# Experts of the last stage in two token halves, the first amid the quantised attention; gates by Tanh and Exp; queries per token tile

## The reference

```python
scores = sigmoid(x_flat @ w_gate); _, topk_idx = top_k(scores, 6)
w = picked scores / their sum
h_r = silu(g_r) * v_r            # g_r, v_r: the halves of x @ w_up of an expert
routed = sum over the 6 of (h_r @ w_down) * w     # tokens beyond an expert's 128th get 0
x = layernorm(x + silu(g_s) * y_s @ w_shared_down + routed)
```

## Time and profile before

| | before |
|---|---|
| three timed runs, median (lowest to highest) | 472.29 us (471.53 to 473.58) |
| span of the profiled execution | 473.8 us |
| the profiled execution's own time | not given by the page apart from its span |
| PE matmul busy / DVE / ACT / POOL | 388.1 / 303.7 / 215.5 / 118.4 us |
| mean granted TensorE clock | 0.879 |

### The profile page before, as it was taken

One profiled execution on the slowest core, in us unless ns is written; L12 is line 12 of the kernel. 1 busy time (PEld: TensorE's weight loads), 2 busy tenths in 40 slices (PEclk: granted clock), 3 DMA queues, 4 the chain that ended last, 5 costly groups with the idle time before them and its releaser, 6 DMA issues.

```text
span 473.8 us, 6810 instructions
## 1 busy us (share of the span) xinstructions
PE 388.1 (82%) x2387; PEld 225.7 (48%) x2387; DVE 303.7 (64%) x611; ACT 215.5 (45%) x551; POOL 118.4 (25%) x215
## 2 busy tenths in 40 slices
PE   5996969389987999999754867768676998999993
PEld 2645457244434566576532223333344544665572
DVE  4984498959624697878646979989871362132235
ACT  2664221272235765855214789899881311111100
POOL 8248646828460000000080111212110000000002
PEclk9989895779988899999985589998975698999997
DMA  8992110670000000000000999999982004011211
GB/s 244 318 361 25 1 2 1 223 310 1 0 1 0 1 3 0 2 1 1 2 0 13 265 169 172 155 163 173 131 162 51 0 0 143 24 44 49 63 44 44
DMA packets 75521, 39.84 MB, mean 84 GB/s; under 512 B 64160, under 2 KB 71264, under 8 KB 75040
## 3 DMA queue, kind: packets, MB, share of 16 engines
q1 hardware_dynamic: 73184, 39.35, 34.1%
q0 software_dynamic: 2304, 0.07, 1.4%
HBM read 21.58 MB, written 2.88 MB: 52 GB/s over the span
## 4 chain that ended last, share of the span: by engine, by line
PE 53%; DVE 15%; DMA 12%; ACT 10%; issue 5%; POOL 4%; SPq 0%; POOLq 0%; ACTq 0%; DVEq 0%
PE ps L762 27%; ACT area_b L692 7%; PE ps L1162 6%; DMA area_b<-area_b 6%; PE ps L945 5%; PE ps L956 5%; PE ps L975 3%; DMA area_a<-area_b 3%; POOL deltas L490 2%; PE ps L939 2%; DMA area_b<-deltas 1%; DVE area_a L1275 1%; DMA deltas<-entry_w,small 1%; ACT area_a L673 1%; DVE stats L1282 1%
## 5 line engine op out<-in xcount | busy, mean ns | idle before, releaser
L1535 DVE CUSTOM_DVE_ANT_0 area_a<-ps,zero,small 128x1024 f32<-128x1024 f32 x64 | 79.4, 1278 | 9.7 <-ACT area_b L692 5.0
L692 ACT ACTIVATE area_b<-area_a,small 128x1024 int16<-128x1024 f32 x64 | 73.0, 1142 | 11.3 <-DMA area_b<-area_b 5.9
L673 ACT ACTIVATE area_a<-ps,small 128x256 f32<-128x256 f32 (+1 forms) x128 | 51.9, 432 | 31.0 <-DVE small L1426 28.7
L459 POOL TENSOR_SCALAR var_eps<-meanvar 128x1 f32<-128x1 f32 x24 | 6.6, 273 | 225.3 <-DVE meanvar L1283 225.2
L762 PE MATMUL ps<-xT_odd,early 128*128 128x512 f32 x128 | 59.5, 613 | 0.0
L1054 PE MATMUL ps<-area_b 128*128 128x512 bf16 x128 | 45.0, 446 | 13.5 <-DVE small L1535 12.4
L1593 DVE TENSOR_TENSOR area_b<-ps,area_b 128x512 f32<-128x512 f32 x16 | 11.1, 691 | 55.7 <-ACT area_b L737 55.7
L1426 DVE TENSOR_REDUCE small<-ps 128x4 f32<-128x1024 f32 (+1 forms) x24 | 29.3, 1222 | 18.3 <-PE ps L945 18.1
L737 ACT ACTIVATE area_b<-ps 128x512 f32<-128x512 f32 x16 | 9.5, 596 | 67.2 <-PE ps L762 67.2
L762 PE MATMUL ps<-area_b,xT_even 128*128 128x512 f32 x64 | 31.1, 631 | 9.0 <-ACT area_b L650 9.0
L762 PEld LDWEIGHTS ps<-xT_odd,early 128*128 128x128 f32 x128 | 25.0, 197 | 27.1 <-issue 26.6
(11 more groups left out here) (265 smaller groups left out, 667.4 us busy)
## 6 DMA issues: line engine op xcount, KB each, us to landing
early<-in_w_up_dram SPq DMA_DIRECT2D x1, 4096.0 KB, 16.1
area_b<-gates_out SPq DMA_DIRECT2D x16, 256.0 KB, 3.0
deltas<-area_b SPq DMA_DIRECT2D x1, 2112.0 KB, 17.8
area_b<-deltas SPq DMA_DIRECT2D x2, 1024.0 KB, 5.9
area_a<-in_w_down_dram SPq DMA_DIRECT2D x1, 2048.0 KB, 8.5
early<-in_ctxT_dram SPq DMA_DIRECT2D x1, 1024.0 KB, 13.1
early<-in_ctx_dram SPq DMA_DIRECT2D x1, 1024.0 KB, 14.0
early<-in_w_qkv_dram SPq DMA_DIRECT2D x2, 384.0 KB, 5.1
```

The source lines that it names most:

```text
L673: a = act.activation(p1[:, n % 2, x * nk * P:(x + 1) * nk * P], scores1(n)[:, x * nk * P:(x + 1) * nk * P], ACT.Exp, bias=nmx1[:, n % 2, x ...
L692: act.activation(px[:, u % PX, :], sx[:, u % 3, :], ACT.Exp, bias=nbx[:, u:u + 1], accum_out=zx[:, i, h:h + 1]).then_inc(sem("px_ready"), 1)
L1535: dve.tensor_tensor_reduce(sx[:, u % 3, :], bank(2 * (u % 2), 2), zero[:].broadcast_to([P, B * M]), qsc[:, i, h:h + 1], LOWEST, ALU.add, A ...
```

## The change

- **Experts.** The 16 groups are done twice, for tokens 0 to 255 and 256 to 511, so there are 32 groups `k`, each with `up` of four matmuls of 256 columns (both halves in one bank, 4 or 5) and `down` of two (bank 3). They have fixed places in a list of 104 steps that goes on from stage 5's 64 units: `up` of the first half at steps 42 to 57, its `down` at 53 to 68; the second half at 74 to 89 and 84 to 99. In its step PE does the scores, `apply`, the previous tile's division and router, then `down`, then `up`. One step after its `up` follow ACT's tanh and DVE's `combine`, two instructions into a ring `raw_up` of eight. The product with the spread gates (`hide`) goes to POOL, from step 52 on, behind that step's bias.
- **Banks.** Since bank 3 is taken, scores of units from 48 on use three banks: bank 1 is shared by neighbours, so the second score matmul of a unit waits for the maximum of the unit before.
- **Functions.** silu(x) becomes x/2 (1 + tanh(x/2)) with ACT's Tanh, sigmoid 1/(1 + exp(-x)) with ACT's Exp and two DVE instructions. The router works tile by tile, each 10 to 15 steps after the tile's last unit.
- **Queries** are made tile by tile: tile 0's amid stage 4's items, tile 1's product right behind them, the rest of tile 1's and those of tiles 2 and 3 amid the first 17 units (tile 3's copy at 32). Tile 2's and 3's end of stage 4 moves there too. `qTx` is cleared at the kernel's start; `qstack` is made by one DVE instruction per tile.
- **DMA.** `w_down` is loaded at step 42. The gates of a half are stored (step 47, and after the units) and spread by four DMAs of 512 KB each (step 49, and after the units). SP waits for the store in its list, between the transpositions. Units 40, 49 and 58 are no longer transposed by PE and ACT; units 62 and 63 are.

```diff
-AHEAD = 6
...
+W = 2 * P
+UNITS = 64
+NARROW = 48
+UP_AT = (42, 74)
+DOWN_AT = (53, 84)
+HIDE_AT = 52
+RAW = 8
+STEPS = 104
...
         def by_scalar(u):
-            return u % SHARE[1] in SHARE[0]
+            return (u < UP_AT[0] - 3 and u % SHARE[1] in SHARE[0]) or u >= UNITS - 2
+        def halves5(u):
+            if u < NARROW:
+                return 2 * (u % 2), 2 * (u % 2) + 1
+            return u % 2, u % 2 + 1
...
+                def spread_gates(p):
+                    sp.wait_ge(sem("gates_stored"), 16 * (p + 1))
+                    for q in range(4):
+                        if p:
+                            sp.wait_ge(sem("hidden_ready"), NG // 4 * (q + 1))
+                        rows = gates_out[p][:, NG // 4 * q * W:NG // 4 * (q + 1) * W]
+                        sp.dma_start(gate_rows[:, NG // 4 * q:NG // 4 * (q + 1), :].rearrange("p g n -> p (g n)"),
+                                     rows.unsqueeze(0).broadcast_to([HE, EG, NG // 4 * W])).then_inc(sem(f"gate_rows_{q}"), 16)
+                def store_gates(p):
+                    sp.wait_ge(sem("gate1T_ready"), p + 1)
+                    sp.dma_start(gates_out[p].rearrange("e (g n) -> g e n", n=W), gate1T).then_inc(sem("gates_stored"), 16)
+                for u in range(UNITS):
...
+                    if u == 42:
+                        sp.wait_ge(sem("o1_ps"), len(items1) // 2)
+                        load("w_down", w_down, t["w_down"].rearrange("(g p) d -> p g d", p=P))
+                    if u == 47:
+                        store_gates(0)
+                    if u == 49:
+                        spread_gates(0)
+                store_gates(1)
+                spread_gates(1)
...
+            def hide(k):
+                p, g = divmod(k, NG)
+                pool.wait_ge(sem("gated_ready"), k + 1)
+                pool.wait_ge(sem(f"gate_rows_{g // (NG // 4)}"), 16 * (p + 1))
+                if k >= 2:
+                    pool.wait_ge(sem("hidden_used"), k - 1)
+                pool.tensor_tensor(out=hidden[:, k % 2, :], in0=raw_up[:, k % RAW, :], in1=gate_rows[:, g, :],
+                                   op=ALU.mult).then_inc(sem("hidden_ready"), 1)
...
+                        add_bias(u // 2 - 4)
+                    if u >= HX and u % HX == 8:
+                        inverse_deviation(5, u // HX - 1)
+                    if HIDE_AT <= u:
+                        hide(u - HIDE_AT)
+                for k in range(UNITS - HIDE_AT, NG):
+                    hide(k)
+                inverse_deviation(5, TT - 1)
+                for i in range(2):
+                    inverse_deviation(6, i)
+                for k in range(NG, 2 * NG):
+                    hide(k)
+                for i in range(2, TT):
+                    inverse_deviation(6, i)
...
+            def tanh_of(k):
+                act.wait_ge(sem("up_ps"), k + 1)
+                if k >= 2:
+                    act.wait_ge(sem("tanh_used"), k - 1)
+                act.activation(tanh_up[:, k % 2, :], bank(4 + k % 2)[:, W:2 * W], ACT.Tanh, scale=0.5).then_inc(sem("tanh_ready"), 1)
...
-                act.activation(score1.rearrange("p i e -> p (i e)"), bank(7)[:, 0:TT * E1], ACT.Sigmoid).then_inc(sem("score1_ready"), 1)
...
-                    act.activation(silu[:, g % 2, :], bank(g % 2), ACT.Silu).then_inc(sem("silu_ready"), 1)
...
+                    if n in (7, 19):
+                        project(n // 12)
+                    if n in (10, 22):
+                        transpose_x(4, [n // 12])
+                    if n == 12:
+                        queries(0)
+                    if n == 15:
+                        turn_queries(0)
                     if n and n % 2 == 0:
                         apply(n // 2 - 1)
-                turn_z(TT - 1)
-                spread_z(TT - 1)
-                project(TT - 1)
+                queries(1)
+                turn_z(2)
...
+                    two = [0, 1] if u < NARROW or u % 2 == 0 else [1, 0]
+                    for order, half in enumerate(two):
+                        if u < NARROW and u >= 2:
+                            pe.wait_ge(sem("maxx_ready"), u - 1)
+                        if u >= NARROW:
+                            pe.wait_ge(sem("maxx_ready"), u - 1 if order == 0 and u >= NARROW + 2 else u)
+                        mm = pe.matmul(bank(halves5(u)[half]), qTx[:, i % 2, h // 2, P * (h % 2):P * (h % 2) + P],
                                        kTx[:, h // 2, half * 512:(half + 1) * 512], start=True, stop=True)
                     mm.then_inc(sem("sx_ps"), 1)
...
+                def up(k):
+                    p, g = divmod(k, NG)
+                    if k < 2:
+                        pe.wait_ge(sem("pTx_act"), before5(UNITS - 2, True))
+                    else:
+                        pe.wait_ge(sem("gated_ready"), k - 1)
...
+                    rows = slice(P * g, P * (g + 1))
+                    dense(bank(4 + k % 2)[:, 0:W], lambda c: w_up[:, c, 1, rows], tokens(p))
+                    dense(bank(4 + k % 2)[:, W:2 * W], lambda c: w_up[:, c, 0, rows], tokens(p)).then_inc(sem("up_ps"), 1)
...
+                def down(k):
+                    p, g = divmod(k, NG)
+                    pe.wait_ge(sem("hidden_ready"), k + 1)
+                    if g == 0:
+                        pe.wait_ge(sem("in_w_down"), 16)
+                        pe.wait_ge(sem("maxx_ready"), NARROW)
+                        if p:
+                            pe.wait_ge(sem("res6_ready"), 2)
+                    for i in range(2):
+                        mm = pe.matmul(bank(3)[:, i * D:(i + 1) * D], hidden[:, k % 2, i * P:(i + 1) * P], w_down[:, g, :],
+                                       start=g == 0 and i == 0, stop=g == NG - 1, skip_group_check=True)
+                    mm.then_inc(sem("proj6" if g == NG - 1 else "hidden_used"), 1)
+                    if g == 0:
+                        pe.wait_ge(sem("shared_ready"), p + 1)
+                        for i in range(2):
+                            pe.matmul(bank(3)[:, i * D:(i + 1) * D], shared[:, i * P:(i + 1) * P], w_sd[:],
+                                      start=False, stop=False, skip_group_check=True)
...
+                    if u in (49, 81):
+                        share(0 if u == 49 else 1)
+                    for k in range(2 * NG):
+                        if down_step(k) == u:
+                            down(k)
+                    for k in range(2 * NG):
+                        if up_step(k) == u:
+                            up(k)
...
+                def combine(k):
+                    dve.wait_ge(sem("tanh_ready"), k + 1)
+                    if k >= RAW:
+                        dve.wait_ge(sem("hidden_ready"), k - RAW + 1)
+                    STT(out=raw_up[:, k % RAW, :], in0=tanh_up[:, k % 2, :], scalar=1.0, in1=bank(4 + k % 2)[:, W:2 * W],
+                        op0=ALU.add, op1=ALU.mult).then_inc(sem("tanh_used"), 1)
+                    dve.wait_ge(sem("tanh_used"), k + 1)
+                    TTN(out=raw_up[:, k % RAW, :], in0=bank(4 + k % 2)[:, 0:W], in1=raw_up[:, k % RAW, :],
+                        op=ALU.mult).then_inc(sem("gated_ready"), 1)
+                def add_6(p):
+                    dve.wait_ge(sem("proj6"), p + 1)
+                    for i in (2 * p, 2 * p + 1):
+                        TTN(out=res[:, i, :], in0=bank(3)[:, D * (i % 2):D * (i % 2) + D], in1=x_tok[1][:, i, :],
+                            op=ALU.add).then_inc(sem("res6_ready"), 1)
...
+                for u in range(STEPS):
+                    if u + 2 < UNITS:
+                        maximum(u + 2)
+                    if u == 0:
+                        take_z(2)
+                    if u == 1:
+                        normalise(2)
+                    if u == 2:
+                        add(2)
+                        norm_stats(4, 2)
+                    if u == 3:
+                        norm_scale(4, 2)
+                        quantise_queries(1)
+                    if u == 4:
+                        take_z(3)
+                        stack_queries(1)
+                    if u == 5:
+                        normalise(3)
+                    if u == 6:
+                        add(3)
+                        norm_stats(4, 3)
+                    if u == 7:
+                        norm_scale(4, 3)
...
+                            norm_scale(5, i)
+                        if k == 11:
+                            route(i)
+                        if k == 14:
+                            gate(i)
+                    if u in (50, 82):
+                        share(0 if u == 50 else 1)
+                    for k in range(2 * NG):
+                        if up_step(k) + 1 == u:
+                            combine(k)
+                    if u == 73:
+                        add_6(0)
+                        scale_6(0)
+                add_6(1)
+                scale_6(1)
```

(81 more changed lines are left out.)

673 lines of the change are left out of this document (330 added, 343 removed).

## The result

| | before | after |
|---|---|---|
| median of the timed runs (lowest to highest) | 472.45 us (471.53 to 473.58, 4 runs) | 491.49 us (488.86 to 492.98, 4 runs) |
| span of the profiled execution | 473.8 us | 487.1 us |
| mean granted TensorE clock in it | 0.879 | 0.892 |

After takes 1.040 times as long, with a 95% interval of 1.035 to 1.044: slower. Forecast were 456 us, with a range of 441 to 478.

The account below looks back on a forecast made before the run. It took PE to bind in stage 4 and behind the units, DVE, ACT and DMA in stage 5, with a gap between. Terms summed to -15.9 from the 473.8 span, 457.9; 1.5 lower for the median, 456 us, range 441 to 478.

Parts of the forecast that it names:

- Second half ... 16 x (1.72 + 0.86) = 41.3: Second half's ups and downs at PE's pace; with shared expert, gates and waits 49 us for 96.3 before, -47.3.
- the ring's loop: From step 53, maximum, score, apply, down, hide, combine and next maximum form a loop of 4.7 us a step.
- lock-step, slower: Rival, chance 0.12: each up's result needed in its own step, 6 us a step, steps 42 to 57 take 102, total 497.
- Steps 42 to 57, 61 us: Units with first-half ups and downs among them: 61 us for 22.6 before, +38.4.
- 58 to 63, 14: Last units' steps: one more ring step, tile 2's router, maxima and last exponential, 14 us for 13.4, +0.6.
- the ring hardly binds: Rival, chance 0.20: PE and DVE run further ahead, steps 42 to 57 take 49 us instead of 61, total 442.
- Units 0 to 41, +12.3 and +7.4: Units 0 to 15: 35 us for 22.7 before; units 16 to 41: 43.5 us for 36.1, from added query and router work.
- Start, -22.6: Gap between stage 4 and the units filled: first maximum at 238 us, 22.6 us earlier.
- no table load: Steps 42 to 57: Tanh shares Exp's set, so no loads; rival with loads, chance 0.05, +13 to +21, 475 us.
- w_down and the spread gates in time: Steps 42 to 57 and second half: DMAs stay beneath, 40 of 61 us; w_down hidden but for 0.5.
- last unit to last tile: Behind the units, to the transposed last tile: PE and ACT transpose, 11.4 us for 13.7 before, -2.3.
- tail: Kernel's end: two tiles' norms instead of four, 6 us, -2.4.

Follow-up runs that it names:

- e1: After with the semaphore count that POOL's product waits on put right in the second half; 479.06 us, ratio 1.010.
- e2: After with a ring of 16 instead of eight, the count left as it was; 485.75 us, ratio 1.026.
- e3: After with both the count put right and the ring of 16; 470.73 us, ratio 0.992.
- e9: e4 with each tile's router on DVE in three parts, a maximum between them, count and gate a step later; 462.72 us, ratio 0.970.
- e6: e4 with the queries' scaling, rounding and stacking for tiles 1 to 3 on POOL instead of DVE; 467.25 us, ratio 0.978.
- e11: e9 with e6's edit alone (queries of tiles 1 to 3 scaled, rounded and stacked on POOL); 461.34 us, ratio 0.977.
- e4: e3 with qTx cleared behind stage 3 instead of at the head of POOL's list; 469.05 us, ratio 0.988.
- e7: Silu in place of Tanh in the experts and shared expert, base kernel not named; 32 loads of 1.283 us, no total time given.
- e10: e4 with e6's queries on POOL, every combine one step later and e9's router in parts; 459.77 us, ratio 0.967.

## Why the prediction was wrong

**The step that failed is "Second half ... 16 x (1.72 + 0.86) = 41.3", sum 49.** It measured 63.6. I took the second half as bound by PE, as before's pairs are the earlier trace rows, and in the ring's loop I wrote that `hide` "has two output buffers and waits for down(k-10)". That holds in the first half. In the second half the semaphore is one short and the two buffers act as one. With the count right (e1) the term is 50.2: the arithmetic was right, the wait overlooked. It is 13.4 of the 14.6 us. No rival had this wait, either: "lock-step, slower" forecast the sign but from a step of over 4.8 us in steps 42 to 57, and there the mean step is 3.7 (maxima of units 44 to 60: 328.5 to 388.3, 16 steps).

The wait is not the whole miss. With the count right e1 still takes 479.06 us and is slower than before: in its trace it is 3.2 us over the forecast at the first maximum (241.22), 7.6 in units 0 to 41 (86.1) and 7.1 from unit 42 to the last exponential (82.1). These terms failed too, in after by 4.2, 4.9 and 5.3 us.

**Steps 42 to 57, 61 us, and 58 to 63, 14.** The ring was there and its loop well sized: five steps, 363.72 to 388.25, take 24.5 us where 24.5 were forecast, with POOL waiting for `down` and `combine` for POOL, and e2 and e3 take it away. That "the ring hardly binds" falls with it. The 5.3 us that are missing lie ahead of the ring (38.2 us to the maximum of unit 55, 36.3 forecast) and behind it (17.5 against 14). Ahead of it the sum lost two units: step u has the maximum of unit u+2, so the steps from 42 on have the maxima of units 44 to 63, and those of 42 and 43, 3.0 us (325.48 to 328.52), are in no term. The steps themselves took 35.2, 1.1 less than forecast. Behind the ring lies tile 2's router, priced at 4.0 on DVE alone; e9 shows that such a block also stops PE for 3.75 us, with a lower clock behind it. This price was left out.

**Units 0 to 41, +12.3 and +7.4.** Measured +9.5 and +15.1, 4.9 us more in sum. Tile 3's quantising, 3.5 us, I had put among the first 16 units; it runs between the maxima of units 16 to 19 (DVE, 278 to 283 us), which moves that much from one term to the other. The rest is waiting. DVE is busy for 43.95 of 51.5 us there, close to the 43.5 that I took for the whole; I had added up DVE's work, 26.8 and 15, and left 1.7 us beyond it. This row stands for the largest, in after's waits from 274 to 326:

```profile
DVE attTx L1767 <- PE ps L1258: 3.7, 2, 2.0
```

PE was working then, but at half clock (0.50 from 284 to 289, the last section's rows, and from 317 to 320). DVE's own work counts as well: 4.9 us less of it gave back 1.5 (e6) to 3.5 (e11).

**Start, -22.6.** -18.4 in after. Of the 4.2 us that are missing, 1.9 are the clearing of `qTx`, to which the forecast gave no price: stage 4 begins at 147.48 for 145.55 in before (e4). The rest differs from one execution to the next: e3, whose code is the same up to there, has -20.9, and in the nine kernels with the clearing moved the first maximum lies between 237.43 and 240.22, for 238.0 forecast.

**Right:** no table load (e7: 15.7 us if there were; 13 to 21 were forecast for it), w_down and the spread gates in time (from 326 us on no engine of after waits for a DMA), last unit to last tile 12.0 for 11.4, tail 5.7 for 6. The forecast of 456 us is 4 to 7 below what the change gives with its count right, a longer ring, the clearing moved and a router in pieces, e10's 459.8 to e9's 462.7. That does not bear it out, since it reckoned with a ring that binds, and theirs does not.

**What stays open:** how much of the clearing's 1.9 us reaches the end; why e6's edit gave 1.5 us beside a whole router and 3.5 beside one in pieces, or whether e6's one trace misleads; and the clock, of which only falls behind idle stretches were seen, none tried by itself.

## What to carry to other kernels

A wait on a count says how many buffers there really are: follow each semaphore past the place where one of its signals goes to another name, and price the loop for the end of the list too, where nothing else hides it. Where three engines take turns on one unit, the sum of each engine's work is only a floor: a block of a few us in one list costs what the others lose behind it, and cutting it up cost nothing here. Moving work into another engine's free time pays only part of its length (here 41 us moved for 11).

## What the runs showed of the hardware

The granted clock fell behind stretches in which PE stood still for a part of the time, and a stall on another engine was so paid twice. In the single downs of after, PE worked 1.13 us and stood 0.95, five times at full clock (2.4 GHz); from 470.2 on the same four matmuls took 2.06 to 2.08 us, half that. Behind tile 3's quantising PE had worked only 1.44 of 5 us, and in the next 5 it was busy all the time at 0.50 (1.2 GHz):

```profile
279.00:284.00 5.00, 1.44 (x19) 0.70 (x20) 4.83 (x12) 3.26 (x7) 0.38 (x2) 0.85 0.85 161
284.00:289.00 5.00, 5.00 (x41) 2.59 (x40) 3.32 (x6) 4.44 (x10) 0.58 (x3) 0.50 0.60 114
```

First PE waited for DVE; then DVE, with PE at half clock, waited for PE.

While POOL cleared 128x4096 bf16 for 3.51 us, DVE stood in the middle of its work: three small instructions that take 0.15 to 0.24 us in e4 lasted 2.80 to 3.02 us in after, and 2.60 to 2.89 in e1 to e3. Beside e4's clearing, from 140.3 on, DVE had one instruction, which reads `ps`, and it took 0.69 us like the one ahead of it. What sets the two apart was not tested.
